# Conditioned residual layers on one core: loads in one queue, a subtraction moved to VectorE, batch 0's product kept in PSUM

## What is computed

```python
# layer 0: low-rank adapted matrix per batch
ae = layernorm(cond, ln_g, ln_b);  h = gelu(ae @ w1 + b1);  xw = h @ w2 + b2
x_a, x_b = split(xw)                      # each (b, 512, 8)
layer = base_layer + einsum('bdr,bkr->bdk', x_a, x_b)
x = x + (x + x @ layer)                   # x @ (layer + 2 I)
# layer 1: modulated and demodulated weight per batch
ys = cond / sqrt(512)
d = rsqrt((ys*ys) @ (W*W) + 1e-8)
x = x + ((x * ys) @ W) * d
```

## Time and profile before

| | us |
|---|---|
| median of 3 runs (320.16 to 321.87) | 321.2 |
| the profiled execution | 320.93 |
| its span, first to last instruction | 318.9 |
| TensorE matmuls busy | 305.3 |
| VectorE, ScalarE, GpSimd busy | 138.5, 134.1, 24.1 |
| mean granted TensorE clock | 0.989 |

### The profile page before, as it was taken

The page is one execution under the profiler, slowest core; times in us unless marked ns, Lnnn a source line. Parts: engine busy times, 40 slices in busy tenths (PEclk is TensorE's granted clock), DMA queues, the critical chain, the costliest instruction groups (busy, mean ns, idle before and its releaser), DMA issues.

```text
span 318.9 us, 3702 instructions
## 1 busy us (share of the span) xinstructions
PE 305.3 (96%) x1442; PEld 236.6 (74%) x1442; DVE 138.5 (43%) x229; ACT 134.1 (42%) x205; POOL 24.1 (8%) x41
## 2 busy tenths in 40 slices
PE   7895999999987999999999999999999999999995
PEld 7563655555665888888888888888888888888884
DVE  3778224243797452561362365523271409131300
ACT  3454132222556363374275275514452445243521
POOL 4350000000051010010010100001000000000000
PEclk9998999999998999999999999999999999999999
DMA  7990379993012436636545565502551155106313
GB/s 203 417 411 32 136 288 377 372 407 136 0 68 66 173 131 211 211 132 199 198 157 185 187 207 192 195 0 85 184 198 61 66 198 199 66 6 194 132 66 132
DMA packets 13728, 54.81 MB, mean 172 GB/s; under 512 B 2048, under 2 KB 2048, under 8 KB 11408
## 3 DMA queue, kind: packets, MB, share of 16 engines
q1 hardware_dynamic: 7920, 36.72, 33.0%
q10 hardware_dynamic: 5792, 17.87, 14.0%
HBM read 37.80 MB, written 16.78 MB: 171 GB/s over the span
## 4 chain that ended last, share of the span: by engine, by line
PE 88%; DMA 4%; DVE 3%; issue 2%; ACT 1%; ACTq 1%; DVEq 0%
PE tile L840 55%; PE tile L720 14%; PE aux L747 10%; PE acc L688 5%; DMA base<-in_w0T 4%; PE aux L737 2%; DVE rs L482 1%; PE aux L803 1%; ACTq L267 0%; DVE rtmp L470 0%; PE acc L777 0%; PE spare L781 0%; DVE rtmp L477 0%; ACT xs L332 0%; ACTq L265 0%
## 5 line engine op out<-in xcount | busy, mean ns | idle before, releaser
L840 PE MATMUL tile<-xs,qs 128*128 128x512 f32 x768 | 179.0, 392 | 2.2 <-issue 2.2
L840 PEld LDWEIGHTS tile<-xs,qs 128*128 128x128 f32 x768 | 145.2, 189 | 32.9 <-issue 2.6
L375 ACT ACTIVATE stream<-tile,dts 128x512 f32<-128x512 f32 x64 | 44.0, 688 | 77.4 <-PE tile L840 77.4
L581 DVE TENSOR_TENSOR xs<-xr,xs 128x1024 fp32r<-128x1024 f32 x32 | 39.0, 1225 | 67.2 <-ACT xs L332 66.6
L720 PE MATMUL tile<-rs,w0s 128*128 128x512 f32 x192 | 48.1, 404 | 3.7 <-ACT base L286 3.7
L720 PEld LDWEIGHTS tile<-rs,w0s 128*128 128x128 f32 x192 | 36.1, 192 | 17.6 <-issue 10.0
L281 ACT CAST rs<-rtmp 128x512 fp32r<-128x512 f32 x32 | 19.9, 621 | 40.3 <-PE tile L720 30.1
L482 DVE TENSOR_TENSOR rs<-rtmp,rs 128x512 fp32r<-128x512 f32 x32 | 23.4, 730 | 30.2 <-ACT rs L281 29.9
L332 ACT CAST xs<-xr 128x1024 fp32r<-128x1024 f32 x32 | 33.3, 1048 | 5.1 <-ACT stream L375 5.1
L747 PE MATMUL aux<-rs,w0s 128*128 128x512 f32 x144 | 34.9, 391 | 0.0
L747 PEld LDWEIGHTS aux<-rs,w0s 128*128 128x128 f32 x144 | 26.8, 188 | 6.2 <-DVE rs L482 0.6
(11 more groups left out here) (107 smaller groups left out, 107.2 us busy)
## 6 DMA issues: line engine op xcount, KB each, us to landing
xr<-in_xT SPq DMA_DIRECT2D x32, 512.0 KB, 3.7
out<-stream ACTq DMA_DIRECT2D x31, 512.0 KB, 2.7
stream<-in_w2u SPq DMA_DIRECT2D x13, 1024.0 KB, 6.5
xr<-in_w2u SPq DMA_DIRECT2D x3, 1024.0 KB, 8.1
base<-in_w0T ACTq DMA_DIRECT2D x4, 256.0 KB, 8.1
w1s<-in_w1n SPq DMA_DIRECT2D x4, 256.0 KB, 5.7
base<-in_wm SPq DMA_DIRECT2D x1, 1024.0 KB, 9.1
base<-in_w0n SPq DMA_DIRECT2D x1, 1024.0 KB, 11.5
```

Of the source, the lines that this page charges most:

```text
L375: nc.scalar.activation(pairs[:, m % PAIRS, o % 2], tiles[n % BANKS][:], ACT.Copy, scale=dts[:, b, o:o + 1]).then_inc(bank_free, 1)
L581: nc.vector.tensor_tensor(xs[:, h, 1, 2 * cp:2 * cp + 2, :], xr[:, cp], xs[:, h, 0, 2 * cp:2 * cp + 2, :].bitcast(F32), ALU.subtract).then ...
L840: last = nc.tensor.matmul(tiles[n % BANKS][:], qs[:, b % 2, u, cc, cols], xs[:, h, v, cc], start=cc == 0 and (u, v) == (0, 0), stop=cc == ...
```

## The change

- SP issues all loads, in this order: cond (now one tensor with the three parameter columns), w1 and w0 chunks 0 and 1 by turns, w1 chunks 2 and 3, w0 chunks 2 and 3, wm, b2, then w2. ScalarE issues no loads.
- w0's low part is subtracted by VectorE (`w0_low`), ahead of `r_low` of the same chunk. GpSimd goes from its constants straight to the 16 casts for perm. In the first product, TensorE does low-by-high ahead of high-by-low.
- The early products are made in the order of batches 1, 2, 3, 4, 0 (`ORDER`). The first four are stored in `base[:, b - 1]`. Batch 0's is the fifth: it stays in `tiles`, its rank part is accumulated on top within chunk kc = 3, and q_high and q_low read `tiles` directly. Its evacuation and its p_sum are gone.
- The correction of the product made first now belongs to batch 1: fix_first(0) and (1) ahead of the main phase, (2) and (3) within p_sum(1, cc). d_spread and its matmuls, and the mask, come later.
- x_high(0, 0, 0) and x_low(0, 0, 0) come behind the copies for the rank part. w2's units are spread as 3, 3, 3, 3, 2, 1, 1 instead of 2, 3, 3, 3, 3, 1, 1.

The diff, cut to its core (`w0_low` is a new function on VectorE that waits for `w0_hi` and subtracts as GpSimd did):

```diff
-W2_AFTER = {(1, 0): 2, (1, 2): 3, (2, 0): 3, (2, 2): 3, (3, 0): 3, (3, 1): 1, (3, 2): 1}
+ORDER = (1, 2, 3, 4, 0, 5, 6, 7)
+W2_AFTER = {(1, 0): 3, (1, 2): 3, (2, 0): 3, (2, 2): 3, (3, 0): 2, (3, 1): 1, (3, 2): 1}
...
-            sp.dma_start(cond[:], condT).then_inc(cond_loaded, 16)
-            for kc in range(KC):
+            sp.dma_start(cond_prm[:], condp).then_inc(cond_loaded, 16)
+            sp.dma_start(w1s[:, 0], w1n[:, 0]).then_inc(w1_loaded[0], 16)
+            sp.dma_start(w0raw[:, 0], w0T[:, 0]).then_inc(w0_loaded[0], 16)
+            sp.dma_start(w1s[:, 1], w1n[:, 1]).then_inc(w1_loaded[1], 16)
+            sp.dma_start(w0raw[:, 1], w0T[:, 1]).then_inc(w0_loaded[1], 16)
+            for kc in range(2, KC):
                 sp.dma_start(w1s[:, kc], w1n[:, kc]).then_inc(w1_loaded[kc], 16)
+            for kc in range(2, KC):
+                sp.dma_start(w0raw[:, kc], w0T[:, kc]).then_inc(w0_loaded[kc], 16)
             sp.dma_start(wms, wm).then_inc(wm_loaded, 16)
+            sp.dma_start(b2s, b2q).then_inc(b2_loaded, 16)
...
-            for kc in range(KC):
-                pool.wait_ge(w0_hi, kc + 1)
-                nc.gpsimd.tensor_tensor(w0s[:, 1, kc], w0raw[:, kc], w0s[:, 0, kc].bitcast(F32),
-                                        ALU.subtract).then_inc(w0_lo, 1)
...
-            for kc in range(2):
-                nc.scalar.dma_start(w0raw[:, kc], w0T[:, kc]).then_inc(w0_loaded[kc], 16)
-            for i, column in enumerate((b1c, lngc, lnbc)):
-                nc.scalar.dma_start(prm[:, i], column).then_inc(prm_loaded, 16)
-            for kc in range(2, KC):
-                nc.scalar.dma_start(w0raw[:, kc], w0T[:, kc]).then_inc(w0_loaded[kc], 16)
-            nc.scalar.dma_start(b2s, b2q).then_inc(b2_loaded, 16)
...
+            w0_low(0)
             r_low(0, 0)
...
             squared_rows(csq, 1, aux[0], 4)
+            x_high(0, 0, 0)
             x_high(0, 0, 1)
             for cc in range(KC):
                 q_high(0, cc)
-            evacuate_base(4)
...
+                if b == ORDER[0]:
+                    if cc >= 2:
+                        fix_first(cc)
                     dve.wait_ge(first_fixed, 3 * cc + 3)
...
+            for kc in range(KC):
+                pe.wait_ge(r_lo, 4 * KC + kc + 1)
+                if kc == KC - 1:
+                    pe.wait_ge(squared, 4)
+                for cc in range(KC):
+                    if kc == 0:
+                        pe.wait_ge(bank_free, 3 * KC + cc + 1)
+                    cols = slice(cc * P, (cc + 1) * P)
+                    for u, v in ((0, 0), (0, 1), (1, 0)):
+                        last = nc.tensor.matmul(tiles[cc][:], w0s[:, u, kc, cols], rs[:, kc, v],
+                                                start=kc == 0 and (u, v) == (0, 0), stop=False)
+                    if kc == KC - 1:
+                        rank_tile(0, cc, start=False).then_inc(tile_done, 1)
+                    elif cc == KC - 1:
+                        last.then_inc(r_used, 1)
+                with_chain(kc)
...
-                        pe.wait_ge(bank_free, n + 1 - BANKS)
+                        if n >= EARLY + BANKS:
+                            pe.wait_ge(bank_free, n + 1 - 2 * BANKS)
+                        else:
+                            pe.wait_ge(p_lo, o + 1)
```

More of the change, by code:

```diff
@@ L338, in q_high @@
             def q_high(b, cc):
-                if b < STORED:
-                    act.wait_ge(p_summed, b * KC + cc + 1)
-                    src = base[:, b, cc, :]
+                if b == 0:
+                    act.wait_ge(tile_done, EARLY - KC + cc + 1)
+                    src = tiles[cc][:]
+                elif b < STORED:
+                    act.wait_ge(p_summed, keep(b, cc))
+                    src = base[:, b - 1, cc, :]
                 else:
-                    act.wait_ge(ac_done, b * KC + cc + 1)
+                    act.wait_ge(ac_done, keep(b, cc))
                     src = aux[cc % 2][:]
@@ L463, in add_two, with w0_low @@
                 nc.vector.scalar_tensor_tensor(blk, ident[:], 2.0, blk, ALU.mult, ALU.add).then_inc(w0_eyed, 1)
+            def w0_low(kc):
+                dve.wait_ge(w0_hi, kc + 1)
+                nc.vector.tensor_tensor(w0s[:, 1, kc], w0raw[:, kc], w0s[:, 0, kc].bitcast(F32),
+                                        ALU.subtract).then_inc(w0_lo, 1)
             def r_scale(b, kc):
@@ L469, in r_scale @@
                     dve.wait_ge(r_lo, n + 1 - RTMP)
[L470 removed]
+                scaled = nc.vector.tensor_scalar(slot, w1s[:, kc], ys[:, ORDER[b], kc:kc + 1], None, ALU.mult)
                 if b == 0:
@@ L509, in _ @@
             step(nc.vector.scalar_tensor_tensor(row(0, B), row(7, B), 1.5, row(5, B), ALU.add, ALU.mult))
+            w0_low(1)
             r_low(0, 1)
@@ L518, in _ @@
                                     ALU.add).then_inc(ae_ready, 1)
+            w0_low(2)
             r_low(0, 2)
@@ L522, in _ @@
             r_scale(0, 3)
+            w0_low(3)
             r_low(0, 3)
@@ L557, in _ @@
             r_low(1, 3)
+            for kc in range(KC):
+                nc.vector.tensor_scalar(d_spread[:, kc], ident[:], dinv[:, ORDER[0], kc:kc + 1], None,
+                                        ALU.mult).then_inc(spread_ready, 1)
+            nc.vector.tensor_reduce(mask[:, 0], sel3[:].rearrange("p q b -> p b q"), mybir.AxisListType.X,
+                                    ALU.add).then_inc(mask_ready, 1)
             r_build(2)
@@ L693, in first_base @@
                 for kc in range(KC):
-                    for u, v in ((0, 0), (0, 1), (1, 0)):
+                    for u, v in ((0, 0), (1, 0), (0, 1)):
                         if (u, v) == (0, 0):
@@ L729, in aux_free @@
             def aux_free(b, cc):
-                n = b * KC + cc
+                n = keep(b, cc) - 1
                 if n >= 2:
-                    pe.wait_ge(p_summed if n - 2 < EARLY else p_lo, n - 1)
+                    pe.wait_ge(*((p_summed, n - 1) if n - 2 < keep(STORED, 0) - 1 else (p_lo, KC + n - 1)))
             def rank_tile(b, cc, start=True):
                 pe.wait_ge(amk_ready, b + 1)
-                nc.tensor.matmul(rank_bank(b, cc)[:], amk[:, b % 2, cc * P:(cc + 1) * P], csq[:, b // 4], start=start,
-                                 stop=True).then_inc(ac_done, 1)
+                return nc.tensor.matmul((aux[cc % 2] if b else tiles[cc])[:], amk[:, b % 2, cc * P:(cc + 1) * P],
+                                        csq[:, b // 4], start=start, stop=True)
             def late_base(b):
@@ L750, in late_base @@
                         last.then_inc(r_used, 3)
-                    rank_tile(b, cc, start=False)
+                    rank_tile(b, cc, start=False).then_inc(ac_done, 1)
             def permute(bank, which, rows):
@@ L818, in with_chain @@
                     permute(aux[0], 3, csp)
-                elif kc == 2:
+            for kc in range(KC):
+                pe.wait_ge(r_lo, 4 * KC + kc + 1)
+                if kc == KC - 1:
                     pe.wait_ge(squared, 4)
-                    pe.wait_ge(first_fixed, 3 * KC)
-                    for cc in range(KC):
-                        rank_tile(0, cc)
-            base_tiles(4, with_chain)
+                for cc in range(KC):
+                    if kc == 0:
[9 more added lines that the diff above has]
+                with_chain(kc)
             for b in range(B):
@@ L869 @@
         "xT": x,
-        "condT": chunked(a["cond_1024"].T),
+        "condp": np.concatenate([chunked(a["cond_1024"].T).reshape(P, -1)]
+                                + [columns(a["L0_cond_" + k]) for k in ("b1", "ln_g", "ln_b")], axis=1),
         "w0T": chunked(a["L0_cond_base_layer"].T),
```

89 lines of the change are left out of this document (36 added, 53 removed).

## The result

The changed kernel takes 308.42 us (median of 4, 307.88 to 308.77) against 320.68 us beside it: 0.961 of the time before, 95% interval 0.958 to 0.965. The forecast was 308.3. The profiled execution took 307.88 us (span 306.1); its mean granted clock is 1.00 where the kernel before had 0.989. One execution of all that follow, of the kernel with merged columns (508.53 us at a mean granted clock of 0.56), was slow and is left out.

What follows compares the result with a forecast made beforehand. TensorE, busy 96% of the span, bounds the kernel, so only its waits and slow clock can be won: 5.5 + 1.7 + 3.7 + 1.7 = 12.6 off 320.93 gives 308.3 us; range 306.2 to 311.9.

Steps and rivals of the forecast that it cites:

- Second product at 22.4: Start: the second product begins at 22.4 us instead of 27.89, a gain of 5.5 us.
- VectorE's list: Start: VectorE's steps, added up from add_two(0) at 5.08 us, reach z at 20.3 and set the second product's start.
- 0.3 taken for perm's casts: Start: GpSimd's 16 casts, moved to 3.1 to 6.3 us, delay VectorE by 0.3 us, within bounds of 0 to 1.
- w0_low on VectorE: Start: four w0_low add 2.4 us to VectorE, but the GpSimd subtractions (1.29 us each) that stretched its subtractions are gone.
- shared the DMA engines with wm and five pieces of w2: Start: w0's loads shared engines with these; putting all weight pieces first lands the last w0 piece between 8 and 10 us.
- the load order brings nothing: Rival, start: w0 lands as late as now, the second product begins near 27.9 with slow clock, 315.5 us; chance 0.05.
- The gap ahead of the second product: Start: TensorE stands idle about 2.2 us there instead of 3.74, and the clock's 1.7 us loss is taken as gone.
- its floor: Start: TensorE's own work ends at 20.0 to 20.2 us; as a rival bound it gives 306.2 us, chance 0.08.
- The 0.30 for the falling clock: Rival, start: the clock still falls behind the gap at 20 to 22 us, costing 1.7 us: 310.0 us; chance 0.30.
- The forecast 3.7 us by waits and 1.7 by the clock: End of the products: removed waits gain 3.7 us (0.3 + 0.8 + 2.2 + 0.4), full clock behind them 1.7.
- the evacuation's 2.2 us: Ahead of the first main tile: TensorE's wait for an evacuation behind four q casts, 2.2 us, goes when the product stays in PSUM.
- both half-speed stretches: Behind the waits ahead of the second product and first main tile: 4 us each near half clock, costing 1.7 us each.

Runs made afterwards that it cites:

- the kernel with merged columns: The kernel before, both load queues kept, with the three parameter columns carried in cond's load instead of three DMAs on ScalarE's queue: 318.85 us, 0.989 of before.
- the run with GpSimd's subtraction: The changed kernel with w0's low part subtracted on GpSimd again, ahead of perm's casts, instead of on VectorE: 311.70 us, 0.971 of before.
- the old queues: The changed kernel with w0 and b2 loaded by ScalarE again, and w1, wm and w2 by SP: 309.13 us, 0.963 of before.
- a gap of 3.6 us: The changed kernel with four idle copies on ScalarE ahead of the first product's evacuation: 312.33 us, 0.975 of before.
- late casts: The changed kernel with GpSimd's 16 casts for perm held back until 22 us: 308.89 us, 0.966 of before.
- the run with the end alone: The changed kernel with ScalarE's loads of w0 and b2 and GpSimd's subtraction both restored; only the end of the products and the batch order are new: 312.29 us, 0.973.

## Why the prediction was right, and where it was not

- **Total and marks.** 308.3 against 308.42. Second product at 22.4: 22.37. First main tile at 89.5: 89.41. Clock 1.00 throughout: so.
- **VectorE's list.** r_low(0,3) ends at 14.99 (14.5 forecast: add_two(0) began 0.3 later, for its DMA), the chain for d took 1.9 (2.1), z stands at 20.79. The list added up to 20.3; it was some 0.5 us short, 0.3 of it the later begin. That the mark was met to 0.03 us is luck: 0.3 taken for perm's casts, which don't show, and 0.2 for z's wait made up for it. Adding a list up from the spacings of rows held to 0.5 us over 16 us.
- **w0_low on VectorE.** The step that it costs less than the contention it ends is shown by the run with GpSimd's subtraction: 3.3 us slower, though 2.4 us leave VectorE's list. The contention is not always r_low's: in the kernel before it took 1.36, 0.69, 0.68 and 1.35, and in chunks 1 and 2 a layer-norm step stood behind the subtraction (1.31 and 1.29).
- **The cause of the late w0: half of it.** The step was that the loads of w0 "shared the DMA engines with wm and five pieces of w2". That is one of two conditions; with wm and w2 held back, w0 is in time even behind the columns. The other, the three columns between the chunks, the prediction missed. The change removes both, the second by carrying the columns in cond's load (cond_prm), an edit that the prediction did not weigh, and either would have done. So with the columns merged the old queues cost 0.7 us, not 6. The rival "the load order brings nothing" is refuted in the kernel before, where holding back wm and w2 made the second product 2.1 us earlier; in the changed kernel the order brings 0.7 us.
- **Loads.** w0's last piece landed near 11 us, not between 8 and 10 (issued at 4.5 us, 6.3 to 6.5 to landing); VectorE wanted it at 12.72, so this cost nothing.
- **Perm's casts.** 0.3 us taken, none measured.
- **The gap ahead of the second product.** 2.2 forecast, 1.5 measured: TensorE began at 6.97 instead of 6.7 and ended its work some 0.5 later than its floor, while VectorE's mark was met. All four executions kept the clock; with a gap of 3.6 us all six lost it. The prediction's 2.2 us itself would have been no safe gap: with GpSimd's subtraction (2.15 us in the profile) the mean clock fell to 0.994 in two of four executions. Even with late casts (1.5 us in the profile) it did in two of six. The 0.30 for the falling clock was not too much.
- **The end.** The forecast 3.7 us by waits and 1.7 by the clock: 5.6 together in the run with the end alone, and 12 matmuls take 3.01 us in the second product and 2.88 in the first main tile, instead of 4.3 and 4.6. The prediction put the evacuation's 2.2 us to keeping the product in PSUM; an order of ScalarE's list does that part.
- **Median and profile.** The sum used both half-speed stretches of the profiled execution. Filling them in the kernel before gave 2.1 us on average, not 3.4. The median before moved between 320.1 and 321.1 from one set of executions to the next, a difference that the forecast, made from one profiled execution, could not see. So part of the closeness of 308.3 to 308.42 is luck.

## What to carry to other kernels

Read what lies in a queue between two late transfers, not only who shares the bandwidth: three 2 KB loads in 16-byte pieces cost 2.2 and 3.4 us, two queues 0.7. Take work off a shared port before off a busy list. Where one engine waits for another's evacuation, look at what that engine's list holds ahead of it; here two such orders were worth 1.5 and 2.9 us without touching the arithmetic.

## What the runs showed of the hardware

- Three DMAs of 2 KB in 16-byte pieces took 5.1 to 8.1 us from issue to landing, and two 256 KB loads behind them 10.7 and 13.3 us, while the other queue had loads of 1 MB; with these held back (four of 256 KB were left there) the same took 5.1 to 6.0, and 5.9 and 6.0.
- One queue (SP) moved 245 GB/s on average over the first 12 us of the changed kernel, two queues 281 with the old loads. It was enough for the start: w0's last chunk was in use at 12.72 with no wait.
- With a GpSimd subtraction of 1.3 us beside it, a 128x8 step of VectorE with two SBUF inputs that began with it took 1.31 us for 0.17, and a 128x512 one that began 0.5 us behind it 1.36 for 0.69.
- An idle stretch of TensorE of 2.15 us was followed by 1.2 GHz in the profile of the kernel with GpSimd's subtraction, and 12 matmuls took 4.57 us instead of 3.0; behind one of 1.5 us the 12 took 3.0. Of 14 executions of three kernels with that gap in the profile (the changed one, old loads, late casts), two showed a fall of the mean clock, at a place that no trace shows.
